# Threshold search of a mixture-of-experts router: one expert and token span per partition instead of 32 tokens of all experts, three rounds to a chunk instead of two

## The reference

```
N = 4096 tokens, E = 8 experts, K = 2, EH = 256, SH = 512
z = xf @ proj_w.T + proj_b
s = sigmoid(z) + expert_bias
probs = softmax(log(clip(s, 1e-12)))
topk_w, topk_idx = top_k(probs, 2);  topk_w /= clip(topk_w.sum(-1), 1e-12)
cap = max(int(ceil(ceil(N * K / E) * 1.25)), 1)            # 1280 of 4096 tokens per expert
wmat = where(pair_e[None, :] == arange(E)[:, None], pair_w[None, :], -inf)
kept_w, kept_pair = top_k(wmat, cap)                       # each expert keeps its cap heaviest
y = sum over kept pairs of kept_w * expert_e(x)
sh = gelu(xf @ sh1_w.T + sh1_b) @ sh2_w.T + sh2_b          # the shared expert
x = x + gb * (sh + y)
```

## Time and profile before

| | |
|---|---|
| median of 3 runs | 1360.0 us |
| profiled execution | 1361.32 us |
| its span, first to last instruction | 1359.6 us |
| TensorE busy | 1250.8 us (92%) |
| VectorE busy | 1051.7 us (77%) |
| ScalarE busy | 973.5 us (72%) |
| GpSimd busy | 863.1 us (63%) |
| mean granted TensorE clock | 0.967 |

### The profile page before, as it was taken

The page is one execution under the profiler, slowest core; times in us unless marked ns, Lnnn a source line. Parts: engine busy times, 40 slices in busy tenths (PEclk is TensorE's granted clock), DMA queues, the critical chain, the costliest instruction groups (busy, mean ns, idle before and its releaser), DMA issues. The chain is left out here.

```text
span 1359.6 us, 31896 instructions
## 1 busy us (share of the span) xinstructions
PE 1250.8 (92%) x9674; PEld 824.1 (61%) x9674; DVE 1051.7 (77%) x1947; ACT 973.5 (72%) x2078; POOL 863.1 (63%) x1675
## 2 busy tenths in 40 slices
PE   4899999999999999999999999999985577999997
PEld 4566666656666665666566566666643355776775
DVE  3678878778868887887788778878764995888887
ACT  4677778777767877787777687777763465877776
POOL 2577677766767766786677677676747564444443
PEclk8899999999999999999999999999996698999999
DMA  5000000000000000000000000000002002334441
GB/s 136 2 2 1 2 2 2 2 4 2 2 4 2 2 1 4 1 2 2 4 2 2 4 2 2 2 1 1 2 1 79 0 0 51 109 94 95 91 98 27
DMA packets 53201, 28.60 MB, mean 21 GB/s; under 512 B 8720, under 2 KB 51224, under 8 KB 53016
## 3 DMA queue, kind: packets, MB, share of 16 engines
q1 hardware_dynamic: 51832, 25.99, 7.9%
q10 hardware_dynamic: 1184, 0.40, 0.1%
HBM read 24.16 MB, written 2.23 MB: 19 GB/s over the span
## 5 line engine op out<-in xcount | busy, mean ns | idle before, releaser
L714 ACT ACTIVATE probs<-bank,neg_max 128x512 f32<-128x512 f32 x512 | 347.3, 684 | 223.8 <-DVE neg_max L836 216.1
L836 DVE TENSOR_REDUCE neg_max<-bank 128x1 f32<-128x512 f32 x512 | 329.6, 685 | 142.3 <-PE bank L533 140.6
L573 PE MATMUL bank<-probsT,qkv 128*64 128x512 f32 x1024 | 275.5, 617 | 0.9 <-DVE oT L853 0.9
L533 PE MATMUL bank<-operands 64*128 64x512 f32 x1536 | 249.8, 430 | 1.8 <-ACT probs L714 0.7
L549 PEld LDWEIGHTS T<-ident,probs 64*128 64x128 f32 x4096 | 168.8, 139 | 46.7 <-issue 21.2
L503 PEld LDWEIGHTS bank<-operands,hT_h 128*128 128x128 f32 x254 | 48.3, 190 | 209.9 <-issue 207.2
L549 PE MATMUL T<-ident,probs 64*128 64x64 f32 x4096 | 171.8, 223 | 3.5 <-issue 2.5
L1640 POOL TENSOR_TENSOR hid_l<-gated,hid_h 128x512 fp32r<-128x512 f32 x64 | 89.2, 1394 | 123.8 <-ACT hid_h L1557 123.8
L533 PEld LDWEIGHTS bank<-operands 64*128 64x128 f32 x1536 | 125.8, 186 | 64.3 <-issue 40.1
L987 POOL TENSOR_TENSOR sq<-qkv 128x256 f32<-128x256 f32 x252 | 149.9, 614 | 12.2 <-ACT qkv L693 12.0
L842 DVE COPY probsT<-T 128x1024 f32<-128x1024 f32 x128 | 155.6, 1216 | 0.2
(11 more groups left out here) (237 smaller groups left out, 2368.3 us busy)
## 6 DMA issues: line engine op xcount, KB each, us to landing
probsT<-gate_scratch SPq DMA_DIRECT2D x64, 256.0 KB, 5.0
out<-x_all SPq DMA_DIRECT2D x8, 256.0 KB, 2.4
probsT<-in_L_ffn_fc_w SPq DMA_DIRECT2D x1, 1024.0 KB, 9.0
raw<-in_L_attn_Wq SPq DMA_DIRECT2D x1, 512.0 KB, 4.4
raw<-in_L_attn_Wk SPq DMA_DIRECT2D x1, 512.0 KB, 7.2
raw<-in_L_attn_Wv SPq DMA_DIRECT2D x1, 512.0 KB, 8.4
raw_o<-in_L_attn_Wo SPq DMA_DIRECT2D x1, 512.0 KB, 8.5
probsT<-in_L_ffn_sh_w SPq DMA_DIRECT2D x2, 256.0 KB, 3.0
```

What stands on the lines that cost most here:

```text
L533: last = nc.tensor.matmul(s_bank(hp, 2 * pair + head)[:], own[rows, q, toks], own[rows, k], start=((q, k) == (QH, KH)), stop=(q == QL))
L573: last = nc.tensor.matmul(O_BANK[rows, :], qkv[:, hp % 4, j, cols], probsT[:, hp % 2, head, j], start=(j == 0), stop=(j == NT - 1), skip_g ...
L714: nc.scalar.activation(probs[:, i % 4], s_bank(hp, i)[:], ACT.Exp, bias=neg_max[:, i:i + 1], accum_out=row_sum[:, hp % 2, i:i + 1]).then_i ...
L836: nc.vector.reduce_max(neg_max[:, i:i + 1], s_bank(hp, i)[:], AX.X, negate=True).then_inc(max_done, 1)
```

## The change

The search is turned. `ranked` and the weights are laid out by place and transposed on TensorE (`turn`, L1236), so that a partition holds one expert and a span of 256 tokens, 16 partitions to an expert. A candidate is then one number per partition, and three `tensor_scalar` instructions with `accum_out` (L1392) compare and count at once, 256 elements each. The count matmul takes `same`, a mask of the partitions of the same expert, and has three columns. The number of candidates passed (`digits`) times the value of the digit is the increment (L1396, L1399). `thr_u`, `less_u` and `digits` lie in a PSUM bank. The masks `same` and `earlier` are made on VectorE ahead of the routing (L1345 to L1347). The final marks, the place in line and the gates are computed in the turned layout, so that the gates leave VectorE as they go to memory; the transposes and the copy behind them are gone.

The shared product runs `down` three tiles behind (`LAG2` = 3). Chunk 0 stands ahead of the search, without counts; chunks 1 to 5 have three rounds each, one behind each of the first three tiles; chunks 6 and 7 have none. The shared result is written over `h2_all`. Rows of `gate_scratch` are 256 tokens long instead of 128. On VectorE the 15 rounds are written out, where a loop stood.

TensorE in a middle chunk, before: from one count to the next (`up` of two tiles, and `down` of the tiles two behind).

The diff, cut to its core:

```diff
-                LAG2 = 2
-                FIN_BANKS, COUNT_BANK = bank[4:7], bank[7]
+                LAG2 = 3
+                TURN_BANK, FIN_BANK, STATE_BANK, COUNT_BANK = bank[4:8]
+                rankedT_ps, probT_ps = TURN_BANK[:, 0:ROUTE], TURN_BANK[:, ROUTE:2 * ROUTE]
+                thr_u, less_u = STATE_BANK[:, 0:1].bitcast(U32), STATE_BANK[:, 4:7].bitcast(U32)
+                digits = STATE_BANK[:, 8:9]
                 H2_BANK, Y2_BANK = bank[0:2], bank[2]
...
+                        nc.gpsimd.iota(apart[:], pattern=[[1, P]], base=P, channel_multiplier=-1).then_inc(consts, 1)
...
                             pe.wait_ge(count_in, m + 1)
-                            nc.tensor.matmul(COUNT_BANK[:, 0:3 * E], ones[:], part_count[:].rearrange("p j e -> p (j e)"),
-                                             start=True, stop=True).then_inc(count_out, 1)
+                            nc.tensor.matmul(COUNT_BANK[:, 0:3], same[:], part_count[:], start=True,
+                                             stop=True).then_inc(count_out, 1)
+                        def turn(out, tile):
+                            for h in range(SPAN):
+                                last = nc.tensor.transpose(out[:, h * P:(h + 1) * P], tile[:, h], ident[:])
+                            last.then_inc(turned, 1)
...
-                        def chunk(c):
+                        def chunk(c, first_count=None):
                             for k in range(SHT):
-                                if k % 2 == 0 and not (isinstance(c, int) and SHT * c // 2 + k // 2 >= SEARCHES):
-                                    count(SHT // 2 * c + k // 2)
                                 up(c, k)
                                 if k >= LAG2:
                                     down(c, k - LAG2)
                                 elif not first_chunk(c):
                                     down(c - 1, SHT + k - LAG2)
+                                if first_count is not None and k < ROUNDS:
+                                    count(first_count + k)
...
-                        pe.wait_ge(consts, 3)
                         chunk(0)
-                        with pe.Fori(1, B - 1) as c:
+                        pe.wait_ge(routed, 1)
+                        turn(rankedT_ps, ranked)
+                        turn(probT_ps, weight)
+                        with pe.Fori(1, 1 + SEARCHES // ROUNDS) as c:
+                            chunk(c, ROUNDS * (c - 1))
+                        with pe.Fori(1 + SEARCHES // ROUNDS, B) as c:
                             chunk(c)
-                        chunk(B - 1)
...
                         pe.wait_ge(fin_in, 1)
-                        nc.tensor.matmul(FIN_BANKS[2][:, 0:E], ones[:], part_count[:, 0], start=True, stop=True).then_inc(fin_out, 1)
-                        nc.tensor.matmul(FIN_BANKS[1][:, 0:E * TT], ones[:], equal[:].rearrange("p e t -> p (e t)"),
-                                         start=True, stop=True).then_inc(fin_out, 1)
-                        nc.tensor.matmul(FIN_BANKS[0][:, 0:E * TT], earlier[:], equal[:].rearrange("p e t -> p (e t)"),
-                                         start=True, stop=True).then_inc(fin_out, 1)
+                        nc.tensor.matmul(FIN_BANK[:, 0:2], same[:], in_part[:], start=True, stop=True)
+                        nc.tensor.matmul(FIN_BANK[:, 2:4], earlier[:], in_part[:], start=True, stop=True).then_inc(fin_out, 1)
                         for k in range(SHT - LAG2, SHT):
                             down(B - 1, k)
-                        pe.wait_ge(gates_done, 1)
-                        for h in range(TT * E // P):
-                            last = nc.tensor.transpose(COUNT_BANK[:, h * P:(h + 1) * P],
-                                                       gates[:].rearrange("p t e -> p (t e)")[:, h * P:(h + 1) * P], ident[:])
-                        last.then_inc(gT2_ready, 1)
...
-                        act.wait_ge(gT2_ready, 1)
-                        nc.scalar.activation(gatesT[:].rearrange("p h k -> p (h k)"), COUNT_BANK[:, 0:TT * E],
-                                             ACT.Copy).then_inc(gT2_copied, 1)
...
+                        link(nc.vector.tensor_scalar(digit_u[:], cand_u[:], 2, None, ALU.logical_shift_right))
+                        link(nc.vector.tensor_copy(less_u, digit_u[:]))
+                        link(nc.vector.memset(thr_u, 0))
+                        dve.wait_ge(consts, 4)
                         link(nc.vector.tensor_copy(rev[:], rev_i[:]))
+                        link(nc.vector.tensor_scalar(apart[:], apart[:], E - 1, None, ALU.bitwise_and))
+                        link(nc.vector.tensor_scalar(same[:], apart[:], 0.0, None, ALU.is_equal))
+                        link(nc.vector.tensor_tensor(earlier[:], earlier[:], same[:], ALU.mult))
                         rev_all = rev[:].unsqueeze(1).to_broadcast([P, TT, E])
...
+                        link(nc.vector.tensor_tensor(by_place(weight), in_pairs(t1), in_pairs(t2), ALU.add))
+                        link(nc.vector.scalar_tensor_tensor(out=t1[:], in0=top1[:], scalar=-1.0, in1=top2[:],
+                                                            op0=ALU.add, op1=ALU.add))
+                        nc.vector.tensor_tensor(by_place(ranked), in_pairs(t1), by_place(weight), ALU.add).then_inc(routed, 1)
+                        dve.wait_ge(turned, 2)
+                        link(nc.vector.tensor_copy(rankedT[:], rankedT_ps))
...
                         def search(m):
...
+                            for j in range(3):
+                                last = nc.vector.tensor_scalar((passed, equal, run)[j][:], rankedT[:], cand_u[:, j:j + 1].bitcast(F32), None,
+                                                               ALU.is_ge, ALU.add, accum_out=part_count[:, j:j + 1])
+                            last.then_inc(count_in, 1)
                             dve.wait_ge(count_out, m + 1)
...
+                            nc.vector.tensor_scalar(enough[:], COUNT_BANK[:, 0:3], float(CAP), None, ALU.is_ge, ALU.add,
+                                                    accum_out=digits).then_inc(thr, 1)
+                            dve.wait_ge(thr, 5 * m + 1)
+                            nc.vector.tensor_scalar(inc_u[:], digits, float(2 ** (TOP - 2 * m)), None,
+                                                    ALU.mult).then_inc(thr, 1)
+                            dve.wait_ge(thr, 5 * m + 2)
+                            if m < SEARCHES - 1:
+                                nc.vector.tensor_tensor(cand_u[:], less_u, inc_u[:].to_broadcast([P, 3]), ALU.bitwise_or)
+                            nc.vector.tensor_tensor(thr_u, thr_u, inc_u[:], ALU.bitwise_or).then_inc(thr, 1)
+                            nc.vector.tensor_scalar(digit_u[:], digit_u[:], 2, None, ALU.logical_shift_right).then_inc(thr, 1)
+                            dve.wait_ge(thr, 5 * m + 4)
+                            nc.vector.tensor_tensor(less_u, thr_u.to_broadcast([P, 3]), digit_u[:], ALU.bitwise_or).then_inc(thr, 1)
+                            dve.wait_ge(thr, 5 * m + 5)
+                        for m in range(SEARCHES):
                             search(m)
...
-                        thr_all = thr_u[:].bitcast(F32).unsqueeze(2).to_broadcast([P, E, TT])
...
+                        limit = thr_u.bitcast(F32)
+                        link(nc.vector.tensor_scalar(passed[:], rankedT[:], limit, None, ALU.is_gt, ALU.add,
+                                                     accum_out=in_part[:, 0:1]), wait=False)
+                        link(nc.vector.tensor_scalar(equal[:], rankedT[:], limit, None, ALU.is_equal, ALU.add,
+                                                     accum_out=in_part[:, 1:2]))
+                        nc.vector.tensor_tensor_scan(run[:], ones[:], equal[:], 0.0, ALU.mult, ALU.add).then_inc(fin_in, 1)
+                        dve.wait_ge(fin_out, 1)
+                        link(nc.vector.tensor_scalar(room[:], FIN_BANK[:, 0:1], -1.0, float(CAP), ALU.mult, ALU.add))
+                        link(nc.vector.tensor_tensor(room[:], room[:], FIN_BANK[:, 3:4], ALU.subtract))
+                        link(nc.vector.scalar_tensor_tensor(out=run[:], in0=run[:], scalar=room[:], in1=equal[:],
+                                                            op0=ALU.is_le, op1=ALU.mult))
+                        link(nc.vector.tensor_tensor(run[:], run[:], passed[:], ALU.add))
+                        nc.vector.tensor_tensor(gatesT[:], run[:], probT_ps, ALU.mult).then_inc(gT2_copied, 1)
...
-                        sp.dma_start(gate_rows[:, e].rearrange("p (t k) -> p t k", t=NT),
-                                     scratch_rows[e, bass.ts(b, NT)].partition_broadcast(P)).then_inc(rows_in[e], 16)
+                        sp.dma_start(gate_rows[:, e].rearrange("p (t k) -> p t k", t=NT // SPAN),
```

(5 more changed lines are left out.)

117 lines of the change are left out of this document (35 added, 82 removed).

## The result

The changed kernel takes 1344.83 us (median of 4 runs, 1343.95 to 1345.74) against 1360.08 us beside it: ratio 0.9888 [0.9871, 0.9905], 15.2 us faster. Run once more beside other kernels it came to 0.9907 [0.9890, 0.9923]. The profiled run took 1343.95 us, its span is 1342.2.

The account below looks back on a forecast made before the run. The prediction took VectorE to bound the kernel, in routing and 15 search rounds of 4.52 us. Its terms, -12.9 + 4.8 + 4.4 - 1.5 = -5.2 us, gave 1355 us on the runs' base, range 1345 to 1364.

Parts of the forecast that it names:

- Term 1: Period of a search round: 3.6 us instead of 4.52 (bounds 2.7 and 5.0), over 14 periods -12.9 us.
- Rival (a): Compares and `enough` in the search: their sums cost nothing, 0.6 us less a round, 1346 us; chance 0.18.
- Term 2: Start of the search, from mask steps and routing to the first count: +4.8 us (bounds +1.5 and +8).
- Term 3: From the last count to the gates, with nine tiles still to come: +4.4 us (bounds +3 and +6).
- Term 4: The gates' way to the experts, loads in pieces of 1 KB instead of 512 B: -1.5 us (-3 to 0).
- (b): Accumulating compares in the search wait for GpSimd once a round, +1.3 us on 14 rounds: 1373 us; chance 0.07.
- (c): The shift of `digit_u` waits for GpSimd in every round, +12 us: 1367, or 1361 in half; chance 0.12.
- (d): TensorE falls to 1.2 GHz in the search rounds, 5.7 us for two tiles, +8.5 us: 1363; chance 0.08.

Follow-up runs that it names:

- four_compares: Changed kernel with a fourth summing compare of 256 elements in each round, its sum unread; expected +5 us, measured +10.
- search_alone: Only the turned search, in the tile order of the kernel before; 4.6 us ahead of the changed kernel up to the block's end, its ratio not above it.
- state_sbuf: Changed kernel with `thr_u`, `less_u` and `digits` in SBUF tiles instead of PSUM; +7.6 us (sum).
- plain_compares: Changed kernel with three compares that write no sums and one reduce behind them; 1366.7 us in all, 21.8 us more behind the attention.

## Why the prediction was wrong

**Term 1 failed in its size.** The mechanism was right, VectorE's chain with an uncovered count. Forecast were 3.2 us of steps and 0.4 of waiting, 3.6 together; measured are 2.76 us of steps, and 2.91 in all over 14 rounds. Piece by piece, forecast against the round at 1069.50: three compares 1.6 / 1.28, count and answer 0.5 / 0.48, `enough` 0.3 / 0.27, `inc_u` 0.2 / 0.19, `cand_u` to the shift 0.18 / 0.14, shift and `less_u` 0.42 / 0.40. So 0.32 of the 0.44 is in the compares. I added 0.1 for each sum, between nothing and ScalarE's 0.197, and 0.06 for the limit per partition; the read lies beside the next compare, so that only the last one's 0.08 us is paid, and the step from one to the next is 0.40.

The wait of the shift was put at 1.2 us in one round of three. In the changed kernel it is 0.1 in one round of three and 0.56 in the first round. What lengthens the third round of a chunk instead is TensorE's two tiles, 3.12 us against 2.76, a share of 0.12 a round. That the wait exists, `four_compares` shows; with rounds of 3.16 us it comes at just the rate and length that I had counted for 3.2. The two errors were one: with compares 0.3 us shorter the beat changes, and the shift falls near the end of a `hid_l` or into the gap between two.

14 x (3.60 - 2.91) = 9.7 us, which is the whole difference between the measured -22.7 and the forecast of -12.9. Rival (a), the sums that cost nothing, had named 3.0 us and 1346, with a chance of 0.18, and came closest.

**Term 2** (+4.8) came out at +5.2, with parts that partly cancel. The masks took 1.27, 1.19 and 1.33 us, and the cast of `rev` ahead of them, now beside a split, 1.17 where it had 0.17: 5.2 late at the first routing step against the 4.0 forecast. The routing itself got 1.4 us shorter, where I had 0.6. From `ranked` to the first count it is +1.4, as forecast. **Term 3** (+4.4) at +4.7, with ScalarE's last copy last, and the room step waiting as described. **Term 4** (-1.5) at -0.8, which is less than that column scatters among kernels with the same gates' way (9.18 to 10.78), so that no gain is shown. The gates' load is no shorter, and `gate_cols` takes 6.84 us from issue to use against 7.56 before, but 7.67 in `search_alone` with the same transfers.

**The rivals.** (b) is excluded, (c) and (d) are real but not in this kernel's beat. None of them said that the order of the tiles itself gives away 4 to 5 us; term 3 held the size, and I took it as the price of the search instead of asking which of the two streams, rounds or tiles, ought to set the pace.

## What to carry to other kernels

Where two engines pass a small result back and forth beside a third, work out each round as a chain and then shift it by a few tenths: a step that can wait for GpSimd is dear or free by its place in the beat, and here one end in PSUM, or an accumulated output, took it out of the game. When the latency chain and the filler work share an engine, spread the chain over all of the filler so that both end together, and send what the next stage needs as soon as it exists, not behind a barrier. Compare profiles from a common event onward, or chance ahead of the change is counted as its effect.

## What the runs showed that I had not expected

A compare of 256 elements is faster without a sum (0.27 us from start to start) than with one (0.40), and yet costs up to 1.42 us in the trace with `hid_l` beside it, while the summing one never passes 0.481. The shift of three numbers took 0.16 us from SBUF to SBUF with GpSimd idle, 1.26 with it busy, and 0.15 out of PSUM in either case. Where the rounds left TensorE pauses of 1.8 to 3.4 us (`four_compares`, `state_sbuf`, `plain_compares`), stretches of 3 to 7 us with matmuls at 0.43 us a step instead of 0.23 followed behind some of them, so a wait on VectorE can cost twice. And the same attention code ended anywhere in a window of 4.7 us from one execution to the next.
